# A selective scan between two MoE passes: gated values kept by token class, dt*u and B by blocks of tokens

## The reference

```
raw, gate = split(layernorm(x) @ W_in)
h   = silu(conv(raw) + conv_b)                  # 4 taps along the sequence
ts, B, C = split(h @ W_x)                       # 64, 16, 16
dt  = softplus(ts @ W_dt + b_dt)
dA  = exp(dt[..., None] * A);  dBu = dt[..., None] * B * h[..., None]
state_t = dA_t * state_{t-1} + dBu_t;  y_t = sum_n state_t[n] * C_t[n]
x  += ((y + h * D) * silu(gate)) @ W_out
```

## Time and profile before

| | |
|---|---|
| device time, median of 3 runs | 800.65 us (798.1 to 801.97) |
| span of the profiled execution | 795.9 us |
| device time of the profiled execution | not given apart from its span |
| busy: TensorE, VectorE, ScalarE, GpSimd | 685.0 (86%), 607.8 (76%), 442.2 (56%), 490.3 (62%) us |
| 128 scans on VectorE | 285.9 us |
| 127 products with C on GpSimd | 305.6 us |
| 8192 matmul instructions of dB*u on TensorE | 153.7 us |
| 128 matmul instructions of the output projection | 32.4 us |

### The profile page before, as it was taken

How to read it: one execution, slowest core, us unless ns; L and a number is a source line. 1 busy time by engine, 2 the same in 40 slices (tenths; PEclk the granted TensorE clock), 3 DMA queues, 4 the chain that set the end, 5 groups by cost and what they waited for, 6 DMA issues and landing times. The chain is left out here.

```text
span 795.9 us, 27862 instructions
## 1 busy us (share of the span) xinstructions
PE 685.0 (86%) x11782; PEld 420.8 (53%) x11782; DVE 607.8 (76%) x1042; ACT 442.2 (56%) x925; POOL 490.3 (62%) x308
## 2 busy tenths in 40 slices
PE   6539999978968999899998989999989439999957
PEld 2524556548644445464554655464546334556547
DVE  7993555536698999899999999989897974555525
ACT  2301555534678878888897997867523102444420
POOL 3004666520248999989999999999961005666520
PEclk8858999999969999999999999999996758999979
DMA  8997998626354441344445143542008805998538
GB/s 275 397 327 211 376 371 301 195 75 262 92 125 109 124 122 36 104 108 138 108 123 120 45 129 78 138 108 57 3 3 293 342 1 168 363 382 276 167 121 318
DMA packets 86087, 141.08 MB, mean 177 GB/s; under 512 B 8340, under 2 KB 33566, under 8 KB 84689
## 3 DMA queue, kind: packets, MB, share of 16 engines
q1 hardware_dynamic: 81552, 126.99, 51.0%
q0 software_dynamic: 4416, 12.39, 4.3%
HBM read 112.02 MB, written 27.57 MB: 175 GB/s over the span
## 5 line engine op out<-in xcount | busy, mean ns | idle before, releaser
L1343 POOL TENSOR_TENSOR BIG<-BIG,R 128x1024 f32<-128x1024 f32 x127 | 305.6, 2435 | 18.5 <-DVE BIG L1266 13.8
L1266 DVE TENSOR_TENSOR_SCAN BIG<-BIG,ps 128x1024 f32<-128x1024 f32 x128 | 285.9, 2270 | 18.4 <-PE ps L896 17.7
L896 PE MATMUL ps<-BIG,stack 64*32 64x128 f32 x8192 | 153.7, 281 | 26.4 <-DVE BIG L1266 21.7
L896 PEld LDWEIGHTS ps<-BIG,stack 64*32 64x32 f32 x8192 | 118.5, 108 | 99.1 <-DVE BIG L1266 66.8
L741 POOL DMA_INDIRECT R<-xn_dram,tok_idx x64 | 65.2, 1019 | 91.1 <-DVE row_idx L674 71.3
L755 POOL DMA_INDIRECT y_dram<-BIG,row_idx x64 | 64.7, 1010 | 64.5 <-DVE BIG L698 57.0
L683 DVE COPY BIG<-ps 128x512 f32<-128x512 f32 x64 | 44.3, 691 | 70.3 <-PE ps L518 70.3
L390 ACT ACTIVATE BIG<-BIG 128x512 f32<-128x512 f32 x64 | 40.4, 631 | 97.1 <-DVE BIG L690 97.1
L1140 ACT ACTIVATE BIG<-R,An 128x510 f32<-128x510 f32 x128 | 84.1, 708 | 5.0 <-DVE BIG L1266 4.9
L1140 ACT ACTIVATE BIG<-BIG,An 128x510 f32<-128x510 f32 x128 | 83.7, 708 | 0.2
L918 PE MATMUL ps<-BIG,fold 128*32 128x512 f32 x512 | 68.8, 611 | 0.0
(11 more groups left out here) (173 smaller groups left out, 1018.9 us busy)
## 6 DMA issues: line engine op xcount, KB each, us to landing
BIG<-in_L_ffn_w SPq DMA_DIRECT2D x120, 512.0 KB, 5.8
BIG<-y_dram SPq DMA_DIRECT2D x18, 512.0 KB, 9.3
BIG<-dt_dram SPq DMA_DIRECT2D x32, 256.0 KB, 4.2
R<-c_dram SPq DMA_DIRECT2D x32, 256.0 KB, 7.2
R<-dt_dram SPq DMA_DIRECT2D x32, 256.0 KB, 5.0
y_dram<-zeros SPq DMA_DIRECT2D x3, 2048.0 KB, 16.2
y_dram<-zeros SPq DMA_DIRECT2D x6, 1024.0 KB, 8.3
xn_dram<-R POOLq DMA_DIRECT2D x2, 2048.0 KB, 11.2
```

Of the source, the lines that this page charges most:

```text
L896: last = nc.tensor.matmul(ps[CW * slot:CW * slot + CW, 2 * (st % 2) + b, :] .rearrange("p (g s k) -> p k g s", g=2, k=4)[:, k], dT[q % 2][ ...
L1266: nc.vector.tensor_tensor_scan(state[st % 3], dA[:, st % 6].rearrange("p b g t -> p (b g t)"), ps[:, u:u + 2, :].rearrange("p b n -> p (b ...
L1343: nc.gpsimd.tensor_tensor(prod[st % RP], state[st % 3].rearrange("p (b g t) -> p b g t", b=2, g=2), Cf[q % 2][:, 2 * gp:2 * gp + 2].rearra ...
```

## The change

Class k of tokens is now a block of 64 consecutive tokens of each sequence. GpSimd writes dt*u in the order (k b s), where b is the sequence and s the place in the block; ScalarE copies B and C out of PSUM in that order, C is stored to DRAM by two DMAs that put it back in token order. The transposes read their stationary operand contiguously, and `dbu` writes runs of 64 columns. The gated values get the order (j t): the gate copy reads PSUM with a step of 4 and writes contiguously, `y_out` reads the PSUM sums with a step of 4, and the output projection reads its stationary operand contiguously. x^T is copied by one instruction instead of two.

```diff
@@ mamba_sync
-                    e.dma_start(c_dram[f], bc[NS:2 * NS, :]).then_inc(M("c_stored"), 16)
+                    for bb in range(2):
+                        e.dma_start(c_dram[f].rearrange("n (b k s) -> n b k s", k=4, b=2)[:, bb],
+                                    bc[NS:2 * NS, :].rearrange("n (k b s) -> n b k s", k=4, b=2)[:, bb])\
+                            .then_inc(M("c_stored"), 16)
@@ mamba_tensor
-                return row.rearrange("p (m k) -> p k m", k=4)[:, k]
+                return row.rearrange("p (k m) -> p k m", k=4)[:, k]
...
-                                .rearrange("p (g s k) -> p k g s", g=2, k=4)[:, k],
+                                .rearrange("p (g k s) -> p k g s", g=2, k=4)[:, k],
...
-                                                SG[q % 2][:, h, :].rearrange("p (t j) -> p j t", j=4)[:, j],
+                                                SG[q % 2][:, h, P * j:P * j + P],
@@ mamba_scalar
-                for bb in range(2):
-                    last = nc.scalar.activation(XTp[f % 2][:, bb, KC - 1:].rearrange("d (p j) -> d j p", j=4),
-                                                ps[:, t_bank(f), :].rearrange("d (j b p) -> d b j p", j=4, b=2)[:, bb],
-                                                ACT.Copy)
-                last.then_inc(M("XT"), 1)
+                nc.scalar.activation(XTp[f % 2][:, :, KC - 1:].rearrange("d b (p j) -> d b p j", j=4),
+                                     ps[:, t_bank(f), :].rearrange("d (j b p) -> d b p j", j=4, b=2), ACT.Copy)\
+                    .then_inc(M("XT"), 1)
...
-                nc.scalar.activation(SG[b % 2][:, h, :], ps[:, 6 + h, :], ACT.Copy).then_inc(M("gate"), 1)
+                nc.scalar.activation(SG[b % 2][:, h, :].rearrange("p (j t) -> p j t", j=4),
+                                     ps[:, 6 + h, :].rearrange("p (t j) -> p j t", j=4), ACT.Copy).then_inc(M("gate"), 1)
...
-                nc.scalar.activation(bc, ps[DTR:DTR + 2 * NS, x_bank(b), :], ACT.Copy).then_inc(M("bc"), 1)
+                nc.scalar.activation(bc.rearrange("n (k b s) -> n b k s", k=4, b=2),
+                                     ps[DTR:DTR + 2 * NS, x_bank(b), :].rearrange("n (b k s) -> n b k s", k=4, b=2),
+                                     ACT.Copy).then_inc(M("bc"), 1)
@@ mamba_vector
-                nc.vector.tensor_tensor(SG[q % 2][:, h, :], ps[:, 4 + h, :], SG[q % 2][:, h, :], ALU.mult)\
+                g = SG[q % 2][:, h, :].rearrange("p (j t) -> p j t", j=4)
+                nc.vector.tensor_tensor(g, ps[:, 4 + h, :].rearrange("p (t j) -> p j t", j=4), g, ALU.mult)\
@@ mamba_pool
-                nc.gpsimd.tensor_tensor(DTU[:, h, :], DT[:, h, :], HH[b % 3][:, h, :], ALU.mult)\
+                nc.gpsimd.tensor_tensor(DTU[:, h, :].rearrange("p (k b s) -> p b k s", k=4, b=2),
+                                        DT[:, h, :].rearrange("p (b k s) -> p b k s", k=4, b=2),
+                                        HH[b % 3][:, h, :].rearrange("p (b k s) -> p b k s", k=4, b=2), ALU.mult)\
```

More of the change, by code:

```diff
@@ L779, in mamba_sync @@
                     load_rows(b, 0)
-                    wait(e, "c_stored", 16 * (b + 1))
+                    wait(e, "c_stored", 32 * (b + 1))
                     wait(e, "prod", STEPS * (b - 1))
@@ L1087, in x_parts @@
                 wait(e, "bt_psum", b)
-                wait(e, "c_stored", 16 * b)
-                nc.scalar.activation(bc, ps[DTR:DTR + 2 * NS, x_bank(b), :], ACT.Copy).then_inc(M("bc"), 1)
+                wait(e, "c_stored", 32 * b)
+                nc.scalar.activation(bc.rearrange("n (k b s) -> n b k s", k=4, b=2),
+                                     ps[DTR:DTR + 2 * NS, x_bank(b), :].rearrange("n (b k s) -> n b k s", k=4, b=2),
+                                     ACT.Copy).then_inc(M("bc"), 1)
             def softplus_rest(b, h):
```

## The result

| | before | after |
|---|---|---|
| device time, median | 801.31 us, 4 runs (798.1 to 802.48) | 788.24 us, 4 runs (785.5 to 791.4) |
| ratio, 95% interval | | 0.9843 [0.9813, 0.9872] |
| span of the profiled execution | 795.9 us | 783.8 us |
| granted clock of TensorE, mean | 0.916 | 0.926 |

The kernel is 13.1 us faster; 8.4 were forecast. The direction and the range (786.5 to 800.5) held, the size is half as large again.

A forecast was written before the change was run, and what follows sets the result against it. VectorE sets the scan stage's pace, with TensorE stopping it at one place per block. Gains 2.1 + 4.0 + 2.2 + 0.1 = 8.4 us, from 800.65 to 792.3 us; range 786.5 to 800.5.

The forecast's parts named there:

- Projection, price of one: Output projection on TensorE: contiguous stationary operand brings 3.9 us per block to 1.8, giving back 2.1 us.
- End of the stage: Last projection, alone on the chain: 4.10 us become about 2.0, gain 2.1 us, passed on to the next stage.
- Blocks 6 and 7: Last two scan blocks: VectorE's waits after the projection shrink, 4.0 us gained in all; GpSimd is late next.
- the cap of the prediction: Blocks 6 and 7: GpSimd's 3.0 us of waiting plus 1.0 us for its later last product limit the gain.
- No wait over 0.5 us after the projection: Sign that the forecast is right: in blocks 6 and 7 no wait after the projection exceeds 0.5 us.
- Blocks 1 to 5: Wait at step 15, mostly not due to the projection: 0.45 us gained a block, 2.2 in all.
- Costs taken as nothing: y_out, gate copy, PSUM writes of the dB*dT matmuls, x^T copy and C stores: each priced at 0 us.
- the first (PSUM writes): Rival: the dB*dT matmuls also get faster with contiguous PSUM writes, 3 to 4 us more, 789 us; chance 0.12.
- the second (not the stride): Rival: the projection's 326 ns weight load comes from something other than the stride, 800.5 us; chance 0.06.
- the fourth (VectorE pays): Rival: y_out's strided PSUM read costs VectorE up to 0.72 us each, 11.5 in all, 803.8 us; chance 0.12.
- The third (the clock gives it back): Rival: TensorE's longer pauses lower its clock, about 1 us in each of blocks 1 to 6, 798 us; chance 0.20.
- The prediction's sign for this rival: Sign of the clock falling inside the loop: 6 us stretches in blocks 1 to 6 with a clock under 0.9.

The follow-up runs named there:

- e2: Before with only dt*u, B, C and the dB*dT matmuls' PSUM writes in blocks of 64 tokens, projection still strided: 0.9974 of before.
- e3: Before with only the x^T copy done by one instruction instead of two: 1.0009 of before.
- e5: Before with eight matmuls on ones in TensorE's pause ahead of the last projection: 0.9976 of before.
- e1: Before with only the projection part (gate copy, y_out and output projection in order (j t)): 0.9841 of before.
- e4: After with only the last block's projection strided again, gate copy and y_out to match: 0.9896 of before.
- e6: After with eight matmuls on ones ahead of the last projection: 0.9881 of before.
- e8: After measured again unchanged, on a second chip: 0.9862 of before.
- e9: After with VectorE's last product made to wait for GpSimd's last one: 805.35 us, one run.
- e11: After measured once more unchanged, on a third chip: 0.9853 of before.
- e7: After with the second dt projection moved from step 12 to step 13: 0.9972 of before.
- e10: After with the first sum of half 1 moved from step 12 behind the blocks of step 15: 0.9913 of before.

## Why the prediction was right, and where not

**The terms over all traces.** The table above has one execution of each kernel. Below are the four traces with the projections strided in all blocks (before, e2, e3, e5) and the seven with them contiguous and nothing else moved in the loop (after, e1, e4, e6, e8, e9, e11). Block 1 is counted from the start of the scan of step 15 in block 0 to that in block 1, and so on. The last line leaves out e4, e5, e6 and e9, whose end was changed.

| us | strided, range and mean | contiguous, range and mean | difference | forecast |
|---|---|---|---|---|
| block 1 | 46.5 to 52.3, 50.3 | 45.4 to 51.1, 48.0 | -2.3 | -0.45 |
| blocks 2 to 5 | 183.5 to 184.8, 183.9 | 181.7 to 182.7, 181.9 | -2.0 | -1.8 |
| blocks 6 and 7 | 85.5 to 86.1, 85.9 | 81.3 to 85.5, 83.6 | -2.2 | -4.0 |
| loop in all | 361.9 to 366.5, 365.2 | 355.7 to 363.0, 358.3 | -6.8 | -6.2 |
| last scan's end to L294 | 21.5 to 21.6, 21.5 | 15.3 to 17.6, 16.2 | -5.3 | -2.1 |

Together the last two lines are 12.1 us, which fits the 11 to 13 us of the timed ratios (0.9841 to 0.9862). The loop came nearly as forecast. The surplus stands at the end of the stage.

**Projection, price of one.** Nearly right. The last 16 contiguous matmuls take 2.05 us, and about 2.0 was forecast. Inside a block two halves take 0.98 + 1.09 = 2.07 us, where the prediction had 1.8 from L571, so a block gets back 1.8 us and not 2.1. That the step of 4 words in the stationary operand was the cause is shown by e1.

**End of the stage.** The term of 2.1 is right (2.05), and "the gain is passed on" too, but what stands behind it was left out of the sum, and here is the surplus. The prediction priced the clock at 0 in its sum and looked for its changes only inside the blocks. From the last scan's end to L294, three traces without the projection part and with no filler have 21.5 to 21.6 us, and the three of after 15.3 to 16.6: 5 to 6 us gained where the sum had 2.1. L451 at the high clock level takes 3.70 us, at the low one 7.19. That row stood in the chain of before: ten matmuls with a one-row stationary operand at 0.7 us each, which was a reason to read the clock of that stretch. Which part of the activity ahead decides when the clock falls is open. It is not the length of the last projection (e4), and the pause ahead of it only shifts it (e5). All traces with contiguous projections in blocks 0 to 6 fall at 4.1 us or later, or not at all, and the strided ones without a filler at 2.3 to 2.5; that is a correlation over thirteen traces, no mechanism.

**Blocks 6 and 7.** Too much: 4.0 were forecast. The first pair of traces seems to bear it out, with 86.05 us before and 81.27 after, 4.8 less; but that trace of after is the lowest of seven, and their mean gain is 2.2. What is late next is GpSimd, as forecast. In that shortest trace it waits 0.3 us between 504 and 585, where it had waited 3.7 in the same part of before:

```profile
POOL BIG L1348 <- DVE BIG L1271: 0.3, 1, 0.3
```

In the other six contiguous traces GpSimd is idle for 0.7 to 3.0 us in these two blocks, and in the strided ones for 3.4 to 4.4. So the cap of the prediction was reached once, and otherwise not.

"No wait over 0.5 us after the projection" failed once in after, in block 6 (0.64). The wait of 0.85 stands ahead of the projection, where before had one of 0.99, and has another source: the clock is low from 517.2 to 520.6, and TensorE's matmuls for a scan take 1.96 us there.

```profile
522.60 6.65 DVE L1271 TENSOR_TENSOR_SCAN BIG<-BIG,ps 128x1024 f32<-128x1024 f32 x3 [0.85 <-PE ps L899]
529.88 6.64 DVE L1271 TENSOR_TENSOR_SCAN BIG<-BIG,ps 128x1024 f32<-128x1024 f32 x3 [0.64 <-PE ps L899]
```

**The cost that GpSimd can put in the way.** The prediction said that GpSimd's last product may come 1 us later, and priced it only as a cap. In the first trace of after it is paid elsewhere: VectorE's own last product, reached while GpSimd still has 1.85 us to do, is held and takes 2.93 instead of 1.59. This is not a fixed price of the change: in e8 and e11, the same kernel, the product takes 1.59 and 1.60, as in before.

**Blocks 1 to 5.** 2.2 forecast, 0.45 a block. From the scan of step 15 in one block to that in the next, undisturbed blocks take 45.8 to 45.9 us in the strided traces and 45.4 to 45.5 in the contiguous ones. The mean gain over blocks 2 to 5 is 0.5 a block. Block 1 scatters by 6 us in either kind; most of what e11's loop has too much, 51.1 against 45.4 in e8, is there, and the cause of the scatter is open. The reading that the wait at step 15 belongs to the sum and the dt projection ahead, not to the output projection, held: with the projection contiguous 1.12 of the 1.48 us remained, and moving the dt projection or the sum took most of it away (the waits of blocks 1 to 5 fell to 0.27 to 0.8 and 0.13 to 0.6). That this would give time is refuted for the dt projection by e7, and for the sum e10 shows no gain.

**Costs taken as nothing.** y_out 666 ns, gate copy 597, L899 64 in 1.08, the x^T copy, the stores of C: all right, by trace and by e2 and e3. Of the rivals, the first (PSUM writes), the second (not the stride) and the fourth (VectorE pays) are refuted. The measured 788.24 is nearest to the 789 of the first rival, so a reader of the time alone would have taken the wrong one for proved. The third (the clock gives it back) went the other way at the end of the stage. Inside the loop the clock is low for 20 to 31 us in the strided traces and 17 to 27 in the contiguous ones, so nothing is given back there. The prediction's sign for this rival, a stretch of 6 us in blocks 1 to 6 with a clock under 0.9, was a poor one: after has 0.72 in 515 to 521, and before has 0.72 in 518 to 524.

**Ahead of the loop.** 1.5 us of the difference between the first two traces cannot be put down to the change: the first scan comes 43.4 to 43.6 us after the first statistics in two traces of after, in e9, e10, e7 and in e5, which is before with a filler at the end, and 44.9 to 45.2 in before, e1 to e4, e6 and e11. It goes with the clock: in these seven traces, and in none of the other six, the clock falls to the low level 22 to 30 us ahead of the first scan. Why it does so in some executions is open.

So the agreement of -8.4 us up to L451 with the forecast, in the first pair of traces, is partly luck. It holds 1.5 us from ahead of the loop and a last product 1.3 us longer, and neither comes back in the third trace of after. What the change gives by all traces is 6.8 us in the loop, 2.05 in the last projection and, less firmly, some 4 by the clock behind it. In the prediction's sum the terms for blocks 1 to 5 and for the last projection had the right size, the one for blocks 6 and 7 was nearly twice too large (4.0 for 2.2), block 1 gave some 2 us more that its scatter does not let one count on, and the clock at the end of the stage was missing.

## What to carry to other kernels

Give TensorE's stationary operand contiguous elements and let the engine that writes it anyway do the permuting while it reads PSUM: the load costs less and the permuted read nothing. Where a term ends at a stage's edge, read the granted clock of what follows as well, since a slow row there can be the clock's and go with the change. Before moving work to close a wait of 1 us, look at which VectorE instructions have two SBUF operands and where GpSimd stands then; in e7 a shift of one dt projection raised their mean from 1.5 to 2.5 us, and one of them to 4.86. And read a term in several executions before calling it confirmed: here the first pair alone had blocks 6 and 7 at twice their mean gain.

## What the runs showed of the hardware that was not expected

- A weight load of fp32 128x128 with a step of 4 words takes 326 ns in the projection and 209 in a transpose; contiguous 191 and 141 (e8). PSUM writes with the same step cost nothing (281 and 281 ns).
- PSUM reads with a step of 4 words cost nothing on VectorE (666 against 665 ns) or on ScalarE (mean 592 against 593); ScalarE's writes to SBUF with that step cost more than twice as much per element (658 ns for 256, 583 for 512 without it).
- The exclusion works both ways. GpSimd in after, beside VectorE's two diagonal products of B (416.66, 1.49 us, and 420.27, 1.20 us), where these forms otherwise take 2.37 and 1.26 us:

```profile
415.80 1.26 POOL L1355 TENSOR_TENSOR state_more<-state_more,BIG 128x512 f32<-128x512 f32 x1
417.03 3.36 POOL L1348 TENSOR_TENSOR BIG<-BIG,R 128x1024 f32<-128x1024 f32 x1
420.34 2.28 POOL L1355 TENSOR_TENSOR state_more<-state_more,BIG 128x512 f32<-128x512 f32 x1
```

VectorE's product at 416.66 is held until 417.06, and GpSimd's at 417.03 until that has ended at 418.15: 1.1 us + 2.3 is the 3.36 shown. About 2 us of GpSimd time per block go this way, and in before no less: its trace has 3.37 and 2.26 us at 419.03 and 422.35.
